# A graph layer with attention on one core: empty slots become row numbers of a cleared row, and a batch's queries and results move as 32 rows or as all

## What is computed

```python
h = relu(layernorm(x))                       # 6250 x 256
q = (h @ Wq + bq).reshape(n, 8, 32) * 32**-0.5
k = (h @ Wk + bk).reshape(n, 8, 32)
v = (h @ Wv + bv).reshape(n, 8, 32)
s = einsum('ehd,ehd->eh', q[src], k[dst])    # one score per edge and head
p = exp(s - segment_max(s, src)[src])
attn = p / segment_sum(p, src)[src]
out = segment_sum(attn[:, :, None] * v[dst], src)
x = x + out.reshape(n, 256) @ Wo + bo
h = relu(layernorm(x))
aggr = segment_sum(edge_attr, dst)           # 100000 x 256, summed by dst
x = x + mlp3(concat(h, aggr))                # W1, W2, W3 with biases
```

## Time and profile before

| | |
|---|---|
| median of three runs | 1770.22 us (1766.67 to 1775.79) |
| the profiled execution's own time | 1770.12 us |
| its span in the profile | 1768.3 us |
| busy: PE, DVE, ACT, POOL | 1466.4, 1508.1, 925.4, 1017.3 us |
| mean TensorE clock granted | 0.916 of full speed |
| bytes moved by DMA | 439.79 MB |

### The profile page before, as it was taken

One profiled execution on the slowest core, in us unless ns is written; L12 is line 12 of the kernel. 1 busy time (PEld: TensorE's weight loads), 2 busy tenths in 40 slices (PEclk: granted clock), 3 DMA queues, 4 the chain that ended last, 5 costly groups with the idle time before them and its releaser, 6 DMA issues.

```text
span 1768.3 us, 26489 instructions
## 1 busy us (share of the span) xinstructions
PE 1466.4 (83%) x6685; PEld 1088.6 (62%) x6685; DVE 1508.1 (85%) x2748; ACT 925.4 (52%) x2790; POOL 1017.3 (58%) x1024
## 2 busy tenths in 40 slices
PE   4699998767888887888888888788888666899998
PEld 4545556546667666766667676666676445566664
DVE  9998887679999889998999899899999997666662
ACT  4744444466566666666656666665663111444442
POOL 6000204977777777777777777777777773422200
PEclk8699999979889999999989899999998887999999
DMA  9022526789999999999999999999999774333321
GB/s 230 9 106 102 200 101 207 234 277 335 342 328 332 328 338 335 340 340 330 336 340 334 327 344 336 339 327 343 324 332 294 230 232 144 108 112 108 107 79 39
DMA packets 237281, 439.79 MB, mean 249 GB/s; under 512 B 47022, under 2 KB 148043, under 8 KB 237121
## 3 DMA queue, kind: packets, MB, share of 16 engines
q0 software_dynamic: 72256, 216.77, 36.6%
q1 hardware_dynamic: 138408, 132.97, 23.1%
q10 hardware_dynamic: 26456, 88.28, 14.1%
HBM read 385.03 MB, written 72.44 MB: 259 GB/s over the span
## 4 chain that ended last, share of the span: by engine, by line
PE 30%; DVE 26%; issue 17%; POOL 15%; DMA 11%; ACT 1%; POOLq 0%; DVEq 0%; SPq 0%; ACTq 0%
POOL U L725 12%; DMA U<-kv_rows,dstb 9%; DVE V L1721 6%; PE bank L1388 4%; PE bank L1096 3%; DVE V L1725 3%; PE bank L1409 2%; POOL EBO L704 2%; PE bank L1097 2%; PE bank L1397 2%; DVE V L1762 2%; PE bank L1371 2%; DVE V L1456 2%; PE bank L1124 2%; PE bank L1209 2%
## 5 line engine op out<-in xcount | busy, mean ns | idle before, releaser
L725 POOL DMA_INDIRECT U<-kv_rows,dstb x856 | 859.1, 1004 | 264.7 <-issue 240.6
L1124 PE MATMUL bank<-EBO 128*128 128x256 f32 x1568 | 394.0, 394 | 18.7 <-POOL EBO L704 7.0
L1124 PEld LDWEIGHTS bank<-EBO 128*128 128x128 f32 x1568 | 303.0, 198 | 75.5 <-issue 16.3
L1209 PE MATMUL bank<-V 128*128 128x264 f32 x1136 | 314.7, 426 | 6.2 <-DVE V L1762 6.2
L1721 DVE TENSOR_TENSOR V<-U,bank_pair 128x1024 f32<-128x1024 f32 x214 | 260.3, 1216 | 60.1 <-DMA U<-kv_rows,dstb 55.7
L861 ACT ACTIVATE EBO<-EBO,ones 128x128 f32<-128x128 f32 x709 | 284.7, 402 | 23.0
L859 ACT ACTIVATE EBO<-iota,dA 128x128 f32<-128x128 f32 x709 | 279.2, 394 | 1.3 <-issue 1.1
L1209 PEld LDWEIGHTS bank<-V 128*128 128x128 f32 x1136 | 242.0, 213 | 54.9 <-DVE V L1762 7.0
L1200 PE MATMUL bank_pair<-V 128*128 128x256 f32 x256 | 92.0, 445 | 120.1 <-DVE V L1721 119.9
L1725 DVE TENSOR_REDUCE V<-V 128x32 f32<-128x1024 f32 x142 | 173.3, 1220 | 4.9
L1762 DVE TENSOR_TENSOR V<-U,bank 128x1024 f32<-128x1024 f32 x142 | 173.0, 1218 | 0.0
(11 more groups left out here) (308 smaller groups left out, 2173.5 us busy)
## 6 DMA issues: line engine op xcount, KB each, us to landing
EBO<-in_edge_attr_dram ACTq DMA_DIRECT2D x163, 512.0 KB
V<-q_rows SPq DMA_DIRECT2D x128, 128.0 KB
EBO<-in_edge_attr_dram SPq DMA_DIRECT2D x31, 512.0 KB
o_log<-R SPq DMA_DIRECT2D x108, 132.0 KB
o_log<-V SPq DMA_DIRECT2D x106, 132.0 KB
U<-kv_rows,dstb POOLq DMA_INDIRECT x856
kv_rows<-U SPq DMA_DIRECT2D x49, 256.0 KB, 2.0
ag_rows<-R SPq DMA_DIRECT2D x98, 128.0 KB
```

Of the source, the lines that this page charges most:

```text
L725: e.indirect_dma_start(out=kvb[:, b % NKV, j, :], out_offset=None, in_=kv_dram[:, :], in_offset=bass.IndirectOffsetOnAxis(ap=dstb[:, k:k + ...
L1124: m = e.matmul(agg_bank(c)[:, 0:D], oh2[i][0:n, j, :], eb[h % NEB][0:n, j % 4, :], start=j == 0, stop=j == 7)
L1209: t = e.matmul(bank[3 + i][:, 0:RW], oho[b % NPV], PV[b % NPV][:, j, :, :].rearrange("p h d -> p (h d)"), start=j == 0, stop=j == 3)
```

## The change

Four things are changed.

1. The table `kv_rows` gets one more row, number `SPARE` = 6272, which POOL clears. An empty slot carries 6272 for its destination, and `gather` has no bound any more, so an empty slot fetches the cleared row.
2. Local numbers count from the batch's first owner (`FL[:, 0, :]`), not from `base`, so that the carry row is row 0.
3. `load_q` and `write_rows` move rows 0 to 31 always, and rows 32 to 127 in a second DMA whose condition `over` SP reads from a new strip `wide`, which DVE works out: 1 where a batch's last owner is 32 or more behind its first. Each semaphore now counts 32 for a batch. `own_carry` and `carries` read row 0.
4. Since rows 32 to 127 of `o_log` are mostly not written any more, ACT clears them beforehand with 27 DMAs, one at the end of each of the tiles 22 to 48 of the projection, each for up to eight batches. Their source is `low`, so ACT waits for POOL to have cleared it (`QZ`). POOL also clears the five query buffers ahead of `low`. DVE, SP and POOL wait for these DMAs (`s_oz`) where they waited for `s_qz`.

```diff
+    SPARE = NP
-        kv_dram = nc.dram_tensor("kv_rows", (NP, 2 * D), F32, kind="Internal").ap()
+        kv_dram = nc.dram_tensor("kv_rows", (SPARE + 1, 2 * D), F32, kind="Internal").ap()
+        NLOW = 32
+        wide = UM.take(NW)[0:1, :].bitcast(I32)
...
+        ZB0, ZBN = 22, 8
+        B_ZERO = 16 * ((NBT - VB + ZBN - 1) // ZBN)
...
@@ load_q, write_rows (SP)
                 r = e.value_load(nqi[0:1, b:b + 1], min_val=0, max_val=NP)
-                e.dma_start(qt[b % NQ], q_dram[bass.ds(r, P), :]).then_inc(s_q[b % NQ], 16)
+                over = e.value_load(wide[0:1, b:b + 1], min_val=0, max_val=1)
+                e.dma_start(qt[b % NQ][0:NLOW], q_dram[bass.ds(r, NLOW), :]).then_inc(s_q[b % NQ], 16)
+                e.dma_start(qt[b % NQ][NLOW:P], q_dram[bass.ds(r + NLOW, P - NLOW), :], cond=over).then_inc(s_q[b % NQ], 16)
 
             def write_rows(b):
+                over = e.value_load(wide[0:1, b:b + 1], min_val=0, max_val=1)
                 e.wait_ge(b_ev, b + 1)
-                e.dma_start(o_log[b * P:(b + 1) * P, :], R[b % NR]).then_inc(s_o[b % NR], 16)
+                e.dma_start(o_log[b * P:b * P + NLOW, :], R[b % NR][0:NLOW]).then_inc(s_o[b % NR], 16)
+                e.dma_start(o_log[b * P + NLOW:(b + 1) * P, :], R[b % NR][NLOW:P], cond=over).then_inc(s_o[b % NR], 16)
...
@@ pool_program
             e.wait_ge(lid_ready, 1)
-            assert pl.on(e.memset(low[:, 0:RW], 0.0)) == QZ
+            e.wait_ge(hist_mm, NHC)
+            for t in qt:
+                pl.on(e.memset(t, 0.0))
+            assert pl.on(e.memset(low[:, 0:2 * D], 0.0)) == QZ
             e.wait_ge(pl.s, QZ)
             e.dma_start(q_dram[NP:NX, :], low[:, 0:D]).then_inc(s_qz, 16)
+            e.dma_start(kv_dram[SPARE:SPARE + 1, :], low[0:1, 0:2 * D]).then_inc(s_qz, 16)
...
                         out=kvb[:, b % NKV, j, :], out_offset=None, in_=kv_dram[:, :],
-                        in_offset=bass.IndirectOffsetOnAxis(ap=dstb[:, k:k + 1], axis=0),
-                        bounds_check=N - 1, oob_is_err=False).then_inc(s_kv[b % NKV], 16)
+                        in_offset=bass.IndirectOffsetOnAxis(ap=dstb[:, k:k + 1], axis=0)).then_inc(s_kv[b % NKV], 16)
...
@@ proj_tile (ACT)
                 e.activation(qb[i][:, :], bq_[:, 0:D], ACT.Copy, scale=SCALE).then_inc(p_qr, 1)
+                b0 = VB + (t - ZB0) * ZBN
+                if VB <= b0 < NBT:
+                    b1 = min(b0 + ZBN, NBT)
+                    e.wait_ge(pl.s, QZ)
+                    e.dma_start(o_log[b0 * P:b1 * P, :].rearrange("(b p) d -> p b d", p=P)[NLOW:P],
+                                low[NLOW:P, 0:RW].unsqueeze(1).to_broadcast([P - NLOW, b1 - b0, RW])).then_inc(s_oz, 16)
...
@@ vector_program
-            e.tensor_copy(nqi[:, :], FL[0:1, 0, :]).then_inc(regs_ready, 1)
+            dv.on(e.tensor_tensor(wide, FL[0:1, 1, :], FL[0:1, 0, :], ALU.subtract))
+            dv.on(e.tensor_copy(nqi[:, :], FL[0:1, 0, :]))
+            e.wait_ge(dv.s, dv.n)
+            e.tensor_scalar(wide, wide, NLOW, None, ALU.is_ge).then_inc(regs_ready, 1)
...
-            step(e.tensor_tensor(lid[:, :], node[:, :], base[:, :], ALU.subtract))
-            step(e.tensor_scalar(lneg[:, :], lid[:, :], 0.0, float(P), ALU.is_lt, ALU.mult))
-            dv.on(e.tensor_tensor(lid[:, :], lid[:, :], lneg[:, :], ALU.add))
+            dv.on(e.tensor_tensor(lid[:, :], node[:, :], fB, ALU.subtract))
```

38 lines of the change are left out of this document (21 added, 17 removed).

## The result

The changed kernel takes **1785.7 us** (median of six runs, 1781.6 to 1786.5) against 1770.7 us of the kernel before in the same session (1766.7 to 1775.8): a ratio of 1.0081, 95% interval 1.0067 to 1.0095. It is slower by 0.8%. The forecast was 1740 us and faster. The time lies inside the range by 0.3 us and 4.3 us from rival 1, and both are luck: in rival 1 the batches gain nothing and the stage ahead of them loses 18.5 us, where the batches gained 35.9 us and that stage lost 46.7.

A forecast was written before the change was run, and what follows sets the result against it. The prediction took POOL's pace of issuing gathers, 5.21 us per batch, to bound the batches. 1770.1 - 50 (batches) + 14.5 (ACT's wait) + 4 (clearings) + 1 (small ones) = 1739.6, so 1740 us, range 1722 to 1786.

The forecast's parts named there:

- rival 1: Gathers: the 0.30 us gap is any gather's start-up and stays, batches keep 5.213 us, 1790 us; chance 0.13.
- The gap before each gather: POOL's gathers: the bound's move into a register causes the 0.30 us gap; without it, 4.0 us per batch.
- -50 us in the batches: Batches: gathers without a bound take 50 us off, at most 55.7 and at least 0.
- The next bound: Batches: once gathers are faster, DVE sets the pace, at 4.95 us per batch.
- The DMA engines' 2.87 us per MB: Batches: DMA engine time per MB, from a share of 0.97 at 338 GB/s; 4.76 us per batch after the change.
- the saved bytes pay for the empty slots: Batches: the 0.197 MB that 32-row transfers save per batch pays for the empty slots' 0.092 MB.
- The 32-row transfers: SP's queries and results: 0.197 MB less per batch, cost going by packet at 47 ns, no gain alone.
- ACT's wait, +14.5: Projection: ACT waits for POOL's clearing, so turn 2 begins at 199.8 us, not 185.25; +14.5 us, bounds 0 and 18.
- The clearings, +4 with bounds 0 and 10: Projection: 27 clearings, 21.7 MB, run beside it at some 345 GB/s; +4 us, bounds 0 and 10.
- SP, 4.3 us per batch with 0.65 to spare: Batches: SP's loads, issues and added work sum to 4.3 us of 4.95, so SP doesn't set the pace.
- The small ones, +1: DVE's setup, SP's first loads and last writes, POOL's extra row: within 2 us either way, taken +1.

The follow-up runs named there:

- e5: The kernel before, with the gathers' bound put into a register once so that no move stands between gathers; 1937.9 us, ratio 0.9917.
- e3: The kernel before with a spare cleared row and gathers without a bound, queries and results still 128 rows, no added clearings; 1734.3 us, ratio 0.9796.
- e6: e3 with three of the four gathers of a batch, leaving out a quarter of the gathered rows; 1710.4 us in one run.
- e8: e3 plus ACT's wait for POOL's clearing at tile 22 of the projection, without the 27 clearings; 1954.7 us, ratio 1.0026 on a slower chip.
- e8b: The same kernel as e8, run again on another chip; 1977.0 us, ratio 1.0036.
- e2: The changed kernel with ACT's clearings begun at tile 27 instead of 22, in 22 larger DMAs; 1782.6 us, ratio 1.0076.
- e12: e3 plus SP's added register loads and two conditional transfers whose condition never holds, no added clearings; 2032.9 us, ratio 1.0412 on a slower chip.
- e1: The changed kernel with the 27 clearings and ACT's wait removed; POOL clears those rows at 45 us in 7 DMAs; 1756.2 us, ratio 0.9913.
- e9b: The changed kernel with clearings that write all 128 rows of a batch from 128 partitions; 2077.8 us, ratio 1.0552 on a slower chip.

## Why the prediction failed, by its steps

- **The gap before each gather: wrong in its mechanism.** The prediction blamed 0.30 us on the move of the bound because two plain DMAs stood end to end. Plain DMAs are another instruction, and they said nothing on the gathers. e5 has no move and the same gap, e3 and the changed kernel too. Rival 1 was right on the gap and wrong on what follows from it, a pace of 5.213 us. What it lacked, and so did I, is that the gather itself gets 51 ns shorter without a bound: 4 x (998 - 947) = 0.204 us per batch, where the batches gained 0.168. The prediction had kept 1.00 us for a gather without a bound, with no row for it. The sign did not hang on this step alone: with the batches' 14.1 us put right and all else as forecast the sum is 1754 us, still faster.
- **-50 us in the batches: mis-sized, -35.9.** The next bound was named rightly: e6 has DVE at 4.936 us, forecast 4.95. But POOL, with its gaps, stayed the bound, at 5.045 us.
- **The DMA engines' 2.87 us per MB: wrong.** From a share of 0.97 at 338 GB/s I took a capacity of 348. e3 runs at 367 at the same pace. The share is no distance to a limit here: it is 0.99 at 292 GB/s in the first stage and 1.00 at 367 in e3's batches. The sentence that the saved bytes pay for the empty slots falls with it.
- **The 32-row transfers: right, they save their bytes.** The batches move 327 GB/s against e3's 367 at one pace. A packet of SP's queue takes 0.166 x 16 x 1782.7 / 98216 = 48 ns, where it took 47; it is only that no time hung on them. By the Trainium skill ("DMA: Bandwidth & Descriptors", section "Rules for kernel authors") one pays mostly overhead for transfers under 64 KB. In the DMA engines' time per packet this trace shows none; what overhead it does show is SP's, in issues.
- **ACT's wait, +14.5: right by itself.** e8 and e8b have 14 to 15 us, and turn 2 came at 201.1 us for 199.8. How much of it the clearings would have hidden in the changed kernel stays open; e2, which was to tell, blocks ACT in another way.
- **The clearings, +4 with bounds 0 and 10: the step on which the forecast failed.** The measured term is 412.0 - 381.5 = 30.5 us on top of the wait. Of these 2 to 4 us are the rest of the setup, since e12, with neither the clearings nor ACT's wait, has its first product at 369.3 us, where e3 has 367.7 and 365.4. With 26 to 29 us in place of 4 the sum is 1762 to 1765 us, which can't be told from no change, even with the batches as forecast. The prediction knew the bytes and took 345 GB/s for them, since POOL's block ran at 319 and PE lost nothing. It took two things from a row of another kind: the rate (that block is 128 rows and partitions wide and gapless, these are 96, at 261 to 299 GB/s), and that a busy DMA system costs PE nothing. The price came through ACT: 63.5 us of waiting for the projection's own stores, two buffers deep, whose landing rose from 1.7 to 7.7 us against the 7.4 us that they have, a path that the prediction does not have, and 14.5 us behind blocked issues, up to 7.4 us each, which it named and took to be hidden. e1 shows the first alone, and in e9b and e2 the second is the larger.
- **SP, 4.3 us per batch with 0.65 to spare: right.** (400 - 53.9) / 79.3 = 4.36 us, room 0.68. A register load took its 0.27 us in the median. The Trainium skill ("DMA: Bandwidth & Descriptors", "Latency and other measured facts") puts it at some 600 ns at least, and this trace doesn't agree. The prediction's sum by that figure counts 2.44 loads, and the program has 3.44, a third for the results' condition. A skipped transfer took 0.10 us, with its arithmetic 0.24 to 0.30 us and not 0.47; time between SP's instructions made up for it. But so small a room is a risk and not a comfort: it is what the other chips take away.
- **The small ones, +1: mis-sized.** The tail costs 3.6 us. SP's added work stands in series behind ACT's last copies there, and I hadn't followed the last batch. The setup ahead of the batches costs 2 to 4 us more (e12, above).

Together: -35.9 + 46.7 + 3.6 = +14.4 us of span, where the prediction had -50 + 18.5 + 1. The first stage explains 28 us of the difference, the batches 14, the tail 3.
